# The second biases of a mixture-of-experts layer: one fp32r product of 100 stacked rows in place of fp32 on 34 rows

## The reference

```python
x = x + xattn(ctx, layernorm(x))              # conv, SiLU, selective scan, gate
x = x + ffn(layernorm(x))

# ffn: 2 shared experts and 32 routed ones; each maps 256 -> 176 -> 256
def _expert_apply(xf, w1, b1, w2, b2):
    return jnp.maximum(xf @ w1 + b1, 0.0) @ w2 + b2
logits = flat @ router_w + router_b
topk_p, topk_i = jax.lax.top_k(softmax(logits), 6)
topk_p = topk_p / jnp.sum(topk_p, axis=-1, keepdims=True)
gates  = zeros.at[arange, topk_i].add(topk_p)                     # T x 32
out = sum_shared(expert(x)) / 2 + sum_routed(gates[:, e] * expert_e(x))
```

## Time and profile before

| | us |
|---|---|
| median of 3 executions | 386.52 |
| the three | 386.78, 384.69, 386.52 |
| the profiled execution | 384.17 |
| its span in the trace | 382.4 |
| PE busy | 358.6 |
| DVE busy | 261.6 |
| ACT busy | 216.7 |
| POOL busy | 201.9 |
| the chain that ended last: share on PE | 84% |

### The profile page before, as it was taken

How to read it: one execution, slowest core, us unless ns; L and a number is a source line. 1 busy time by engine, 2 the same in 40 slices (tenths; PEclk the granted TensorE clock), 3 DMA queues, 4 the chain that set the end, 5 groups by cost and what they waited for, 6 DMA issues and landing times.

```text
span 382.4 us, 6892 instructions
## 1 busy us (share of the span) xinstructions
PE 358.6 (94%) x2301; PEld 320.4 (84%) x2301; DVE 261.6 (68%) x449; ACT 216.7 (57%) x539; POOL 201.9 (53%) x159
## 2 busy tenths in 40 slices
PE   6456889999999999999999999999999999999997
PEld 4233567898999898989999889989999899999996
DVE  3479988899988467499977556899763634344444
ACT  2867755768754445378644456496423346566662
POOL 0479998369993102389961011799830034444442
PEclk9959899999999999999999999999999999999999
DMA  7498871468523215897322235965232144233310
GB/s 233 133 329 240 214 239 44 117 220 283 162 76 87 68 53 136 252 287 206 97 79 82 63 122 155 338 196 141 82 84 82 43 141 139 82 86 89 106 57 27
DMA packets 30751, 54.20 MB, mean 142 GB/s; under 512 B 3298, under 2 KB 8580, under 8 KB 30724
## 3 DMA queue, kind: packets, MB, share of 16 engines
q1 hardware_dynamic: 30724, 53.86, 47.7%
HBM read 52.54 MB, written 1.31 MB: 141 GB/s over the span
## 4 chain that ended last, share of the span: by engine, by line
PE 84%; DMA 5%; DVE 5%; POOL 3%; ACT 2%; issue 1%; SPq 0%; DVEq 0%; POOLq 0%; ACTq 0%
PE acc L549 36%; PE z L570 12%; PE z L571 12%; PE z L572 12%; PE dA L549 4%; DMA bt<-bc 3%; PE acc L447 2%; DVE dA L777 1%; POOL w1l L916 1%; PE acc L556 1%; POOL bu L936 1%; PE misc L469 1%; DMA stage<-in_w 1%; PE dA L483 1%; PE dA L478 1%
## 5 line engine op out<-in xcount | busy, mean ns | idle before, releaser
L549 PE MATMUL acc<-hg,w 128*128 128x256 f32 x564 | 133.5, 379 | 0.0
L702 ACT ACTIVATE z<-z,par 128x256 f32<-128x256 f32 x188 | 75.7, 439 | 86.4 <-PE z L572 86.4
L570 PE MATMUL z<-xh,w1l 128*128 128x256 f32 (+1 forms) x376 | 118.5, 315 | 0.0
L936 POOL TENSOR_TENSOR bu<-bt,du 128x512 f32<-128x512 f32 x64 | 81.0, 1277 | 60.1 <-DMA bt<-bc 43.7
L549 PEld LDWEIGHTS acc<-hg,w 128*128 128x128 f32 x564 | 102.4, 190 | 11.2
L877 DVE TENSOR_TENSOR hg<-z,gt 128x512 f32<-128x512 f32 x88 | 60.5, 688 | 67.7 <-ACT z L702 66.9
L572 PE MATMUL z<-xh,w1h 128*128 128x256 f32 (+1 forms) x376 | 106.2, 282 | 0.0
L571 PE MATMUL z<-xl,w1h 128*128 128x256 f32 (+1 forms) x376 | 105.9, 282 | 0.0
L777 DVE TENSOR_TENSOR_SCAN dA<-dA,bu 128x512 f32<-128x512 f32 x64 | 78.2, 1222 | 9.7 <-POOL bu L936 8.9
L570 PEld LDWEIGHTS z<-xh,w1l 128*128 128x128 f32 x376 | 71.2, 189 | 5.9 <-issue 4.3
L571 PEld LDWEIGHTS z<-xl,w1h 128*128 128x128 f32 x376 | 70.7, 188 | 1.6
(11 more groups left out here) (130 smaller groups left out, 404.1 us busy)
## 6 DMA issues: line engine op xcount, KB each, us to landing
w<-in_w SPq DMA_DIRECT2D x92, 256.0 KB, 2.8
bt<-bc SPq DMA_DIRECT2D x32, 256.0 KB, 5.3
ct<-bc SPq DMA_DIRECT2D x32, 256.0 KB, 6.0
stage<-in_w SPq DMA_DIRECT2D x11, 512.0 KB, 6.8
gt<-gates SPq DMA_DIRECT2D x14, 128.0 KB
xr<-in_xr SPq DMA_DIRECT2D x4, 256.0 KB, 5.8
x<-in_xT SPq DMA_DIRECT2D x4, 256.0 KB, 5.0
out<-x SPq DMA_DIRECT2D x3, 256.0 KB, 7.0
```

The costliest lines, as they stand in the source:

```text
L549: mm = pe.matmul(total(b, k), weights, h, start=t + n == 0 and (k == 0 or final_batch(b)), stop=last, skip_group_check=True)
L570: pe.matmul(z[p % ZB][:, i, :], w1l[:, t, one], xh_, start=k == 0, stop=False)
L702: ins = act.activation(z[p % ZB][:, i, :], z[p % ZB][:, i, :], ACT.Relu, bias=b1[:, t:t + 1])
L936: pool.tensor_tensor(bu[:, r, :].rearrange("p (j l) -> p j l", j=2), bt[:, c % BRING], du[:, k:k + 1, :].broadcast_to([P, 2, L]), ALU.mult ...
```

## The change

The fp32 product of 34 rows becomes one fp32r product of 100 rows. The biases are loaded as three copies of the 32 routed rows and two of the two shared rows. Rows 0 to 31 and 64 to 95 of the new tile `b2F` hold the rounded biases, rows 32 to 63 the remainders, rows 96 and 97 the rounded shared biases, and 98 and 99 their remainders. On the other side, rows 0 to 63 of `gF` hold the rounded gates, rows 64 to 95 their remainders, and the last four 1/2. One product so gives the sum of three.

```diff
+NB2 = 3 * NR + 2 * NSH
+GLOW_AT = 2
...
-        small = sb("small", [NR + NSH, DX])
+        small = sb("small", [NB2, DX])
...
-        g34 = sb("g34", [P, 2, NR + NSH])
-        gT = sb("gT", [NR + NSH, L])
+        g34 = sb("g34", [P, 2, NB2])
+        gT = sb("gT", [NR, L])
+        gF = sb("gF", [NB2, L], F32R)
+        b2F = sb("b2F", [NB2, DX], F32R)
...
-                        mm = pe.matmul(misc[0:NR + NSH, 1, t * P:(t + 1) * P], g34[:, t, :], ident, start=True, stop=True)
+                        mm = pe.matmul(misc[0:NB2, 1, t * P:(t + 1) * P], g34[:, t, :], ident, start=True, stop=True)
...
                 if p == B2_AT:
-                    for k in range(KD):
-                        pe.matmul(total(b, k), b2x[:, k * P:(k + 1) * P], gT[:], start=False, stop=False,
+                    pe.wait_ge(S["glow_done"], b + 1)
+                    for k in range(KD):
+                        pe.matmul(total(b, k), b2F[:, k * P:(k + 1) * P], gF[:], start=False, stop=False,
...
+                elif name == "b2h":
+                    act.activation(b2F[:], small[:], ACT.Copy).then_inc(S["b2h_done"], 1)
+                elif name == "b2s":
+                    act.wait_ge(S["b2l_done"], 2)
+                    act.activation(b2F[3 * NR:3 * NR + NSH, :], small[3 * NR:3 * NR + NSH, :], ACT.Copy).then_inc(S["b2h_done"], 1)
...
-                    act.activation(gT[:], misc[0:NR + NSH, 1, :], ACT.Copy).then_inc(S["gates_done"], 1)
+                    act.activation(gT[:], misc[0:NR, 1, :], ACT.Copy)
+                    act.activation(gF[:], misc[0:NB2, 1, :], ACT.Copy).then_inc(S["gates_done"], 1)
...
+                elif name == "b2l":
+                    dve.wait_ge(S["b2h_done"], 1)
+                    for rows in (slice(NR, 2 * NR), slice(3 * NR, NB2)):
+                        dve.tensor_tensor(b2F[rows, :], small[rows, :], b2F[rows, :].bitcast(F32),
+                                          ALU.subtract).then_inc(S["b2l_done"], 1)
...
-                        ins = dve.tensor_scalar(g34[:, t, 0:NR], em[:, t, :], rsm[:, t:t + 1], None, ALU.mult)
+                        ins = dve.tensor_scalar(g34[:, t, 0:3 * NR].rearrange("p (o n) -> p o n", o=3),
+                                                em[:, t, :].rearrange("p (o n) -> p o n", o=1).broadcast_to([P, 3, NR]),
+                                                rsm[:, t:t + 1], None, ALU.mult)
...
+                if p == GLOW_AT:
+                    dve.wait_ge(S["gates_done"], b + 1)
+                    dve.tensor_tensor(gF[2 * NR:3 * NR, :], misc[2 * NR:3 * NR, 1, :], gF[2 * NR:3 * NR, :].bitcast(F32),
+                                      ALU.subtract).then_inc(S["glow_done"], 1)
```

More of the change, by code:

```diff
@@ L76 @@
 HEAD = [(("warm", None, 11), 0), ("xin", 0), (("warm", None, 16), 0), ("cv0", 0), (("taps", 1, KC), 0), (("warm", "conv_done", 6), 0), ("econv", 0), ("uclip", 0),
-        (("warm", "uclip_done", 8), 0), ("usig", 0), ("w1h", 0), ("w1l", 0), (("warm", "usig_done", 4), 0), ("u", 0), ("stats", 0), ("xall", 0),
-        ("dtl", 0), ("w1h", 0), ("w1l", 0), ("dt", 0), ("sp", 0), ("over", 0), ("rs1", 0), ("w1h", 0), ("delta", 0), ("nb1", 0)]
+        (("warm", "uclip_done", 8), 0), ("usig", 0), ("b2h", 0), ("w1h", 0), ("w1l", 0), (("warm", "usig_done", 4), 0), ("u", 0), ("stats", 0), ("b2l", 0), ("xall", 0),
+        ("dtl", 0), ("b2s", 0), ("w1h", 0), ("w1l", 0), ("dt", 0), ("sp", 0), ("over", 0), ("rs1", 0), ("w1h", 0), ("delta", 0), ("nb1", 0)]
 HEAD += [(("bu", 0, _k), 0) for _k in range(KD)]
@@ L141, in xattn_ffn_kernel @@
         dtw = pv("dtw")[NBC:NXA, :]
-        b2x = small[:]
         ones = sb("ones", [P, L], BF16)
@@ L216, in xattn_ffn_kernel @@
         aexp_done, aneg_done, const_done = sem("aexp_done"), sem("aneg_done"), sem("const_done")
-        names = ["xin_done", "conv_done", "econv_done", "u_done", "xall_done", "dtl_done", "bc_spilled", "dt_done", "abs_done", "wide_done", "half_done", "half_added", "spread_done",
+        names = ["xin_done", "conv_done", "econv_done", "u_done", "xall_done", "dtl_done", "bc_spilled", "dt_done", "abs_done", "b2h_done", "b2l_done", "glow_done", "wide_done", "half_done", "half_added", "spread_done",
                  "v_done", "sp_done", "delta_done", "zz_done", "ez_done", "zmul_done", "bu_done", "da_ready",
@@ L1017 @@
     put("ident", np.eye(P, dtype=f32))
-    small = np.zeros((NR + NSH, DX), f32)
-    small[:NR] = ff["rb2"]
-    small[NR:] = ff["sb2"]
+    small = np.concatenate([ff["rb2"]] * 3 + [ff["sb2"]] * 2, axis=0).astype(f32)
     arrays = {
```

## The result

| | before, us | after, us |
|---|---|---|
| median | 386.52 (384.69 to 387.10, 6 runs) | 382.23 (382.11 to 382.66, 6 runs) |
| ratio to before | | 0.9901, 95% interval 0.9877 to 0.9925 |
| profiled execution | 384.17 | 382.66 |
| its span | 382.4 | 380.8 |

The kernel after is faster by 1.0% (0.75 to 1.2%), or 3.8 us by the ratio. The forecast was 381.4, in a range from 378.8 to 384.9. Right behind the predicted gain stands one oddity: the two profiled executions are only 1.6 us of span apart, and after's executions lie within 0.6 us of each other, where before's spread over 2.4.

What follows compares the result with a forecast made beforehand. From 70 us on TensorE's stream was taken to bound the kernel, before 52 us the first batch's scan on DVE and its transfers. Terms -4.0 - 1.2 + 0.1 = -5.1 from the median 386.52 gave 381.4, range 378.8 to 384.9.

Steps and rivals of the forecast that it cites:

- The biases: Bias product in each batch: two fp32r records, 0.24 us, no entering or leaving losses; 1.01 us saved each, 4.0 in all.
- The turning: Turning product L517, weights from 34 to 100 columns: 0.31 us saved in each of four turnings, 1.2 in sum.
- the losses stay: Rival: 100 of 128 is still partial, so both products keep entering and leaving losses; -1.9 us, 384.6; chance 0.13.
- only one of them goes: Rival: only rows or only columns matter, so one product keeps its losses; -3.5 us, 383.0; chance 0.12.
- fp32r's speed: Rival: the bias product in fp32r runs as slowly as fp32, 0.86 for 0.24 us; 383.9; chance 0.03.
- "b2l" starts when DVE's statistics end at 13.77 and ends at about 14.65.: Start, DVE: the two subtractions for the biases' remainders, at most 0.43 us each.
- start: Added bias splitting on ACT and DVE and a larger load, mostly covered before POOL's first product: +0.1 us, bounds 0 and 1.0.
- 0.35 later is 315.84, which just fits.: Batch 3: the gates' remainder subtraction on DVE delays `final` without making TensorE wait; zero, bound 0.1 us.
- the start isn't covered: Rival: POOL's first product waits for du or the longer transfer queue, moving the scan up to 1.0 us; 382.3; chance 0.06.
- The gates' way: Wider DVE writes, a second ACT copy, later store and reload of gates: zero, bound 0.3 us in each of three batches.
- Slower: Rival: a shifted start moves a clock drop to 1.2 GHz behind 59 us, where TensorE sets the time; 388.5; chance 0.04.

Runs made afterwards that it cites:

- the filled kernels: Before, its 34 rows and columns filled with zeros, all fp32: to 100, 382.16 us; to 66, 383.48 us; to 64, 387.61 us (one execution).
- the other trace: Before, unchanged, profiled once more: 386.07 us, ratio 1.0013; its profiled execution took 385.75 us.
- the subtraction last: After, with the subtraction of the rounded gates moved behind DVE's other work of pair 2: 380.94 us, ratio 0.9872.

## Why the prediction was right, and where it was off

**Right in size by its first terms.** The biases: 3.40 us from layer to layer in batches 0 to 2, as forecast, and 329.44 - 326.34 = 3.10 in batch 3. The gain of 4.0 us is exact. The turning: 0.44 and 0.12 against a forecast 0.45 and 0.12, 0.3 us each, 1.2 in all. The reading that both losses belong to partly filled operands, taken on nearness alone, is now shown by the filled kernels: 66 rows behave like 100, and 64 like 34. That it was a step at half the array, and not a cost of anything short of 128, the prediction couldn't know; there it was a guess that came true. The rivals by which the losses stay, or only one of them goes, are out, and so is that of fp32r's speed. One reading was loose: around few columns the loss on entering is 0.12 to 0.13 us (0.56 and 0.99, where full ones take 0.44 and 0.86), not the 0.20 of few rows; the 0.2 on leaving is the same.

**Off by two terms.** The forecast was -5.1; the ratio gives -3.8.

*"b2l" starts when DVE's statistics end at 13.77 and ends at about 14.65.* It took 2.70 us, not 0.86. I took 0.43 us from L832, which ran while POOL did nothing, for an operation with two SBUF inputs that I had placed myself beside POOL's w1l subtraction. The term "start" was +0.1 with a bound of 1.0; at POOL's first product it was +2.0, beyond that bound.

*0.35 later is 315.84, which just fits.* The new subtraction on DVE took its 0.42 us, but it pushed `hl` from just ahead of POOL's subtraction to just behind it. The term was 0 with a bound of 0.1, and measured 1.1 us of TensorE's wait.

**Why it came out inside the range all the same.** The lost 2 us of the start didn't reach the median, for the head that I had read in before's profile was a lucky one. The clipping took 1.52 us there and 3.51 in the other trace. With a stream of 307.5 and the 1.8 us outside the span, before's medians of 385.95 to 386.52 give a head of 76.6 to 77.2 by estimate, and after's is 76.5 to 77.0. From the median: stream -3.7, head about 0. The late clipping alone explains 76.4; whether the clock's fall makes the rest isn't shown, for no trace of before has it. The rival "the start isn't covered" happened, at twice its price, and was paid for by this. That was luck: nothing in the prediction weighed the one against the other, and from the profile it was built on the forecast of 379.1 was missed by 3.6 (382.66). I had asked why the profiled execution lies 2.35 us under the median only to shift the level; the answer began with a row in that very profile, a 128x512 operation of 1.52 us that took 0.42 in the other batches.

The gates' way cost nothing that the wait list shows, as forecast. In the profiled execution of after the clock cost nothing: its mean was 0.978, 0.982 before, and no slice behind 59 us is below 9. But what the rival "Slower" feared, a fall behind 59 us, did happen in three other traces of this case, for 1.0 us each. The later reload of the gates isn't in TensorE's wait list. A rest of 0.2 us in the stream (302.8 with the subtraction last, against 307.5 - 4.97 = 302.6) stays open.

## What to carry to other kernels

Look at the rows and columns of every small product: in this kernel one of 34 or 64 cost 0.1 to 0.2 us on entering and 0.2 on leaving, beside full ones, and zeros up to 66 took both away. Before an operation with two SBUF inputs is put on DVE, look at what POOL does at that time, and at what the shift does to the operations behind it; one operand in PSUM avoids the meeting. And where the profiled execution and the median differ, look in the profile for an operation whose duration isn't that of its kind, before a change is costed against either.

## What the runs showed of the hardware

A DVE operation that waits behind POOL shows as a longer duration, not as a wait: 2.25 us in place of 0.42, 1.28 in place of 0.41, 3.51 in place of 0.42, each ending 0.28 us after POOL's, and 1.44 in place of 0.17, ending 0.03 after it. The wait lists don't name POOL for any of them. Between two POOL operations that follow each other without a pause DVE sometimes gets in and sometimes doesn't, at the same place of the same program: 1.52 us in one execution and 3.51 in the other. With this gone, executions that had spread over 3.5 us (17 of 18) lay within 1.7. Behind the longer holding-up TensorE idled, and in three traces its clock then fell to the level of 1.2 GHz from about 67 to 71 us, which cost 1.0 us more; in two others (before's second and fp32 with 100 rows) it idled as long and the clock stayed. The lost gap also means that a delay can make a kernel steadier: after, 2 us late, spreads over 0.6.
